# A Gram product without its lower left block, which is transposed from the upper right one a slot later

## The reference

```python
q = _conv1x1(Wq, bq, y).reshape(B, H, Dh, -1)
k = _conv1x1(Wk, bk, y).reshape(B, H, Dh, -1)
v = _conv1x1(Wv, bv, x).reshape(B, H, Dh, Lx)
scores = jnp.einsum('bhdl,bhel->bhde', q, k) / jnp.sqrt(jnp.float32(E))
out = jnp.einsum('bhde,bhel->bhdl', softmax(scores), v)
o = Wo @ out + bo + x            # then a group norm over the whole sample
```

## Time and profile before

| | us |
|---|---|
| median of 3 runs | 1660.42 (1659.11 to 1662.01) |
| profiled execution | 1660.06 |
| its span, first to last instruction | 1658.2 |
| TensorE matmul busy | 1564.0 (94%) |
| VectorE busy | 1335.9 (81%) |
| ScalarE busy | 989.7 (60%) |
| GpSimd busy | 470.9 (28%) |
| mean granted clock of TensorE | 0.989 of full |

### The profile page before, as it was taken

One profiled execution on the slowest core, in us unless ns is written; L12 is line 12 of the kernel. 1 busy time (PEld: TensorE's weight loads), 2 busy tenths in 40 slices (PEclk: granted clock), 3 DMA queues, 4 the chain that ended last, 5 costly groups with the idle time before them and its releaser, 6 DMA issues.

```text
span 1658.2 us, 53782 instructions
## 1 busy us (share of the span) xinstructions
PE 1564.0 (94%) x23816; PEld 1311.1 (79%) x23816; DVE 1335.9 (81%) x2006; ACT 989.7 (60%) x1779; POOL 470.9 (28%) x293
## 2 busy tenths in 40 slices
PE   3999999999999999999999999999999999999982
PEld 3888888888888888888888888888888888888872
DVE  1777978879798887978879798887978879798883
ACT  2566576575655666576575656666576575656652
POOL 0113314142232313314142232313314142231313
PEclk9999999999999999999999999999999999999995
DMA  5223232423324233232423314233232423314021
GB/s 212 88 62 103 77 111 66 134 78 115 98 65 128 77 110 104 75 113 66 137 75 116 101 62 128 78 110 103 81 107 69 135 74 116 102 61 128 22 77 51
DMA packets 96182, 158.25 MB, mean 95 GB/s; under 512 B 5328, under 2 KB 38224, under 8 KB 95696
## 3 DMA queue, kind: packets, MB, share of 16 engines
q1 hardware_dynamic: 95952, 154.83, 30.3%
HBM read 121.25 MB, written 33.55 MB: 93 GB/s over the span
## 4 chain that ended last, share of the span: by engine, by line
PE 80%; DVE 12%; ACT 3%; issue 3%; DMA 1%; POOL 1%; SPq 0%; DVEq 0%; POOLq 0%; ACTq 0%
PE pj_ps L278 38%; PE l_ps L278 11%; PE l_ps L382 6%; PE w_ps L313 6%; PE s_ps L302 6%; PE w_ps L331 5%; DVE o_sb L813 2%; PE s_ps L291 2%; PE l_ps L398 2%; PE l_ps L418 2%; ACT o_sb L570 1%; DVE row_max L691 1%; ACT y_hi L521 1%; DVE yt_hl L677 1%; DVE prob L698 1%
## 5 line engine op out<-in xcount | busy, mean ns | idle before, releaser
L895 POOL TENSOR_TENSOR prob<-prob,row_inv 128x1024 f32<-128x1024 f32 x128 | 259.8, 2030 | 980.1 <-DVE row_inv L708 980.1
L580 ACT CAST att_hi<-w_ps 128x256 fp32r<-128x256 f32 x256 | 82.6, 376 | 254.0 <-PE w_ps L331 249.8
L278 PE MATMUL pj_ps<-y_hi,w_hi 128*128 128x512 f32 x512 | 208.5, 407 | 3.7 <-DVE y_lo L673 3.7
L278 PE MATMUL pj_ps<-y_lo,w_hi 128*128 128x512 f32 x512 | 202.5, 395 | 0.0
L278 PE MATMUL pj_ps<-y_hi,w_lo 128*128 128x512 f32 x512 | 202.3, 395 | 0.0
L691 DVE TENSOR_REDUCE row_max<-s_ps 128x16 f32<-128x1024 f32 x128 | 156.0, 1218 | 47.3 <-PE s_ps L302 46.2
L703 DVE TENSOR_REDUCE row_sum<-prob 128x16 f32<-128x1024 f32 x128 | 154.9, 1210 | 45.5 <-ACT prob L562 45.5
L557 ACT COPY prob_t<-w_ps 128x512 f32<-128x512 f32 x256 | 149.8, 585 | 39.3 <-PE w_ps L313 35.7
L313 PE MATMUL w_ps<-cst,prob 128*128 128x128 f32 x1024 | 147.7, 275 | 19.9 <-DVE att_lo L715 19.1
L912 POOL TENSOR_TENSOR o_sb<-o_sb,u_sb 128x1024 f32<-128x1024 f32 x64 | 165.8, 2612 | 1.6 <-ACT o_sb L570 1.6
L698 DVE TENSOR_TENSOR prob<-s_ps,row_max 128x1024 f32<-128x1024 f32 x128 | 155.5, 1215 | 0.1
(11 more groups left out here) (105 smaller groups left out, 3576.0 us busy)
## 6 DMA issues: line engine op xcount, KB each, us to landing
y_raw<-in_ctx SPq DMA_DIRECT2D x64, 512.0 KB, 4.9
yt_raw<-in_ctx_t SPq DMA_DIRECT2D x64, 512.0 KB, 4.1
x_raw<-in_x SPq DMA_DIRECT2D x64, 512.0 KB, 4.8
out_z<-o_sb SPq DMA_DIRECT2D x64, 512.0 KB, 3.4
mask_b<-in_mask SPq DMA_DIRECT2D x64, 256.0 KB, 3.8
u_sb<-in_w SPq DMA_DIRECT2D x1, 2048.0 KB, 10.7
w_sb<-in_w SPq DMA_DIRECT2D x1, 1024.0 KB, 13.7
cst<-in_consts SPq DMA_DIRECT2D x1, 512.0 KB, 5.3
```

The costliest lines, as they stand in the source:

```text
L278: last = mm(dst, lhs, rhs, start=i == 0, stop=i == len(todo) - 1)
L895: nc.gpsimd.tensor_tensor(cut, cut, row_inv[:, u % 2, :].unsqueeze(2).to_broadcast([P, 2 * HEADS, CHUNK]), ALU.mult).then_inc(probs_done, 1)
```

## The change

Three places. (1) Of half i=1, the Gram products leave out the first 128 columns (rows of the second half by columns of the first): 384 columns instead of 512. (2) In slot 5 three blocks of `hl` are transposed and added instead of four, and the additions of slots 4 and 5 cover only the upper blocks, 256 columns of the first half and 128 of the second. (3) In slot 6 the stage of layer 0 is new: TensorE waits for the finished upper blocks (`upper_done`), transposes the upper right block into the free quarter of `l0_ps[0]`, and VectorE copies it to the lower left block of `gram`. `gram_done`, for which T1 waits, now comes from this copy. In `layer0` of VectorE, the stage of slot 6 stands behind the statistics of the previous sample.

```diff
+UPPER = ((0, 0), (0, 1), (1, 1))
                 for lb in range(PAIRS):
+                    hi_lo = yt_hl[:, lb, :, :].rearrange("p a c -> p (a c)")
                     for i in range(HALVES):
-                        last = mm(l0_ps[i][:, :].rearrange("p (a c) -> p a c", a=2), yt_hl[:, lb, 0, i * P:(i + 1) * P], yt_hl[:, lb, :, :],
+                        last = mm(l0_ps[i][:, i * P:], yt_hl[:, lb, 0, i * P:(i + 1) * P], hi_lo[:, i * P:],
                                   start=q == 0 and lb == 0, stop=q == BLOCKS - 1 and lb == PAIRS - 1)
...
                 if s == S_HLT:
                     pe.wait_ge(gram_half, count(n, 1, 0))
-                    for i in range(HALVES):
-                        for k in range(HALVES):
-                            last = nc.tensor.transpose(l0_ps[0][:, i * E + k * P:i * E + (k + 1) * P], hl[:, k, i * P:(i + 1) * P], ident)
+                    for i, k in UPPER:
+                        last = nc.tensor.transpose(l0_ps[0][:, i * E + k * P:i * E + (k + 1) * P], hl[:, k, i * P:(i + 1) * P], ident)
                     last.then_inc(hlt_ready, 1)
+                elif s == S_SUM:
+                    pe.wait_ge(upper_done, count(n, 1, 0))
+                    nc.tensor.transpose(l0_ps[0][:, E:E + P], gram[:, 0, P:E], ident).then_inc(lower_ready, 1)
...
                     for i in range(HALVES):
-                        last = tt(gram[:, i, :], l0_ps[i][:, 0:E], hl[:, i, :], ALU.add)
+                        last = tt(gram[:, i, i * P:], l0_ps[i][:, i * P:E], hl[:, i, i * P:], ALU.add)
                     last.then_inc(gram_half, 1)
                 elif s == S_HLT:
                     dve.wait_ge(hlt_ready, count(n, 1, 0))
-                    tt(gram[:, :, :], l0_ps[0][:, :].rearrange("p (i c) -> p i c", i=HALVES), gram[:, :, :], ALU.add).then_inc(gram_done, 1)
+                    for i in range(HALVES):
+                        last = tt(gram[:, i, i * P:], l0_ps[0][:, i * E + i * P:(i + 1) * E], gram[:, i, i * P:], ALU.add)
+                    last.then_inc(upper_done, 1)
+                elif s == S_SUM:
+                    dve.wait_ge(lower_ready, count(n, 1, 0))
+                    nc.vector.tensor_copy(gram[:, 1, 0:P], l0_ps[0][:, E:E + P]).then_inc(gram_done, 1)
```

More of the change, by code:

```diff
@@ L164, in build @@
         wout_ready, u_done = sem("wout_ready"), sem("u_done")
+        upper_done, lower_ready = sem("upper_done"), sem("lower_ready")
         gram_ready, hl_copied, gram_half = sem("gram_ready"), sem("hl_copied"), sem("gram_half")
```

## The result

The changed kernel takes 1672.8 us in the median of 6 runs (1669.69 to 1675.09), the kernel before in the same runs 1660.26 us (1657.79 to 1662.01). The ratio is 1.0074, with a 95% interval of 1.0060 to 1.0088: slower by 12.5 us, where 12.8 was forecast. The profiled execution took 1673.22 us, 13.2 more than the one before.

What follows compares the result with a forecast made beforehand. TensorE was taken to bound the kernel where it lies on the chain, VectorE not far behind. A 23.7 us loss at T1 less 10.9 us gained gave +12.8 on 1660.06, so 1672.9 us, range 1666.0 to 1678.0.

Steps and rivals of the forecast that it cites:

- What bounds the kernel: TensorE, busy 94%, counts only on the chain, which passes Gram parts q=0, q=2 and q=3 but not q=1.
- Part 1: Half i=1 Gram products: 128 fewer columns save 0.228 us a part, three of four parts counting, 10.9 us gained.
- Part 2: One transpose leaves slot 5 and returns in slot 6: TensorE's transposes sum to zero, with 2.9 us to spare for upper_done.
- Part 3: VectorE's additions: 128 columns cost 0.28 us; slot 4 takes 0.13 us less, slot 5 0.02 us more.
- Part 4: Copy last in VectorE's slot 6 brings gram_done late: T1 waits about 1.58 us in 15 samples, 23.7 us lost.
- extremes of the copy's price: Ends of the range for the slot 6 copy: 0.15 us gives 1667.3 us, 0.345 us gives 1677.5 us, with differing part counts.
- Does it arrive at the end?: Work queued on TensorE behind T1, from slot 7's output projection on, moves by the full 1.58 us.
- rival (a): TensorE's 1.17 us wait in slot 10 swallows the new one: faster, 1655.3 us; chance 0.07.
- VectorE itself loses about 0.2 us in slot 7: VectorE's loss in slot 7 from the copy, claimed well inside the time by which TensorE is later.
- Rival (b): GpSimd's joins end 0.8 us sooner against TensorE, so T1's wait is about half as long: same, 1660.9 us; chance 0.05.
- Rival (c): Gram products don't get shorter, as something other than columns sets their pace: 1683.8 us; chance 0.04.
- Rival (d): The clock falls after the longer TensorE wait, 23 us more, about 1696 us; chance 0.02.

Runs made afterwards that it cites:

- the two half parts: Kernel before with the eight products of Gram part q=1, or in another kernel q=3, cut from 512 to 256 columns: 1659.34 us (q=1), 1644.88 us (q=3).
- the columns alone: Changed kernel without the moved transpose and the copy, gram_done in slot 5 again, lower left Gram block not computed: 1649.75 us, ratio 0.9943.
- all columns in the products: Changed kernel with all 512 columns in every Gram product again, the late copy kept: 1682.78 us, ratio 1.0141.
- the joins-early kernel: Changed kernel with GpSimd's joins one slot earlier, the gram copy still last in slot 6: 1654.97 us, ratio 0.9969.

## Why the prediction was right, point by point

- *What bounds the kernel* held. TensorE's time counts where the chain passes; q=1 is off it and q=3 on it, which the two half parts show directly.
- *Part 1* held: 0.445 ns a column gave 0.228 us a part, and the table has 0.21, 0.23 and 0.23 for q=0, q=2 and q=3, 0.66 to 0.67 in all instead of 0.68; 10.9 us were forecast, the columns alone measured 9.8.
- *Part 2* was wrong in its sum, though it cost nothing here. "TensorE's transposes sum to zero" took the one that leaves slot 5 for a gain. It isn't. With all columns in the products, the scores of layer 1 right behind the transposes of slot 5 start where they did (0.01 us earlier), though a transpose has left. What takes the gain back is ScalarE: these scores start 0.05 us after ScalarE has copied prob_t, before and after. TensorE's idle time before these products, before and after:

```profile
  ACT prob_t L557: 3.3, 15
```

```profile
  ACT prob_t L562: 5.1, 15
```

The 1.8 us more are 0.12 us a sample, the length of the transpose that left. The one that enters slot 6 costs 0.11 us a sample on TensorE. In the changed kernel it lies under the wait for the copy; where the wait is gone it shows.

- *Part 3* held: 128 columns took 0.281 us, forecast 0.28.
- *Part 4* held in mechanism, and in size by terms that err against each other, so it is in part luck that 12.8 came within 0.3 us of the measured 12.5. The copy took 0.27 us, forecast 0.28. From its end to T1 it was 0.05 us, not the 0.14 that I took from another pair of instructions, so T1 moved against the y_sum_b copy by 0.81 + 0.67 = 1.48 us and not 1.58. But T1's eight products then took 1.99 us instead of 1.89, which the prediction didn't have, and by the scores of slot 8 the shift is 0.92 + 0.67 = 1.59. Both extremes of the copy's price, 0.15 and 0.345, are out. TensorE's idle time before T1 is shown as 1.2 us only, since the moved transpose fills 0.11 and the tail of the product before it 0.16.
- *Does it arrive at the end?* Yes, undiminished: +0.92 at the scores, +0.93 when TensorE starts again in slot 10, +0.95 at the next sample, and the wait of slot 10 is 19.1 us as before. So rival (a) is wrong. Its premise, that VectorE's stretch would begin when it did, fails at line 752, where VectorE waits the longer. That wait was to grow to over 1 us and grew to 0.87. The step that failed there is "VectorE itself loses about 0.2 us in slot 7": it reaches line 752 0.59 us later than before. In slot 7 it now stands where it didn't stand before, 0.20 us for att_hi of ScalarE and, ahead of it, for layer 1's scores, which TensorE makes late:

```profile
882.13 1.23 DVE L696 TENSOR_REDUCE row_max<-s_ps 128x16 f32<-128x1024 f32 x1 [0.56 <-PE s_ps L304]
```

As 0.87 us of VectorE's wait were left, all of the delay arrived.

- Rival (b) didn't happen in the changed kernel, but the joins-early kernel is its mechanism made to happen: with the joins out of the way the wait shrinks and the sign turns. Rival (c) is out: a 384-column product is followed by the next after 0.176 us, the pace forecast, against 0.23 us at 512 columns. Rival (d) is out too: the mean granted clock is 0.989 in both profiles.

On the copy: 0.269 us for 128 columns against 0.149 for one gives 0.94 ns a column, the full price and not the half one that line 755 shows within SBUF.
The Trainium skill (VectorE: DVE Perf Modes, "Why PSUM operands drop a tier") says that an operand in PSUM holds fp32 to one element a cycle; the trace agrees, in that the copy has the slope of the PSUM additions.
On the joins: the y_sum_b copy, when it starts during a join, ends 0.15 us behind the join's end, whether it has started early or late. The Trainium skill (SBUF — State Buffer, "shared port pair" under its terms) says that VectorE and GpSimd take turns on one pair of ports, held for a whole instruction; that fits all three lengths, 0.29, 1.36 and 1.54 us. That it is this port was not tried by itself.

## What to carry to other kernels

Where a change moves the signal that another engine waits for, look not at the cost of the added instruction but at the moment at which the signalling engine reaches its new place, against the moment at which the waiter arrives. Here a copy of 0.27 us cost 23 us at the end of VectorE's slot and nothing ahead of the y sums. A transpose that left a place where another engine was waited for gained nothing, and the one that entered elsewhere cost its full 0.11 us. And a saving on the busiest engine is worth what the chain says: the same cut was worth 14.6 us in one part and nothing in the one next to it.

## What the hardware showed that I had not expected

After a wait of any length shown here (about 0.1 to 1.4 us) the eight fp32 products of T1 took 1.99 us from the first start to the last end instead of 1.89, and the work behind them came about 0.11 us later. The loss is all between the first product and the second, 0.32 us apart instead of 0.216, and goes with a first weight load that no longer runs ahead of the product; that the load is the cause was not tried by itself. The time from a VectorE instruction's end to the waiting TensorE instruction was 0.05 us before T1 and 0.14 us before a Gram part. Taking the second figure over to T1 gave an error of 0.1 us.
